# Softmax denominators from products of ones with the transposed probabilities

## The reference, cut to what matters

```
q, k, v = heads(x @ Wq), heads(x @ Wk), heads(x @ Wv)       # 8 heads of 32
scores  = einsum('bhnd,bhmd->bhnm', q, k) / sqrt(32)
scores  = where(adj, scores, -inf)
attn    = softmax(scores, axis=-1)
out     = relu(einsum('bhnm,bhmd->bhnd', attn, v)) @ Wo
x       = layernorm(x + out)
```

## Time and profile before

| | |
|---|---|
| median of three runs | 1895.2 us (1893.5 to 1897.09) |
| span of the profiled execution | 1892.0 us, 40139 instructions |
| mean granted TensorE clock | 0.963 of full speed |
| PE busy | 1672.9 us (88%) |
| DVE busy | 1513.0 us (80%) |
| ACT busy | 1120.7 us (59%) |
| POOL busy | 1314.4 us (69%) |

### The profile page before, as it was taken

One profiled execution on the slowest core, in us unless ns is written; L12 is line 12 of the kernel. 1 busy time (PEld: TensorE's weight loads), 2 busy tenths in 40 slices (PEclk: granted clock), 3 DMA queues, 4 the chain that ended last, 5 costly groups with the idle time before them and its releaser, 6 DMA issues.

```text
span 1892.0 us, 40139 instructions
## 1 busy us (share of the span) xinstructions
PE 1672.9 (88%) x12032; PEld 1482.6 (78%) x12032; DVE 1513.0 (80%) x5366; ACT 1120.7 (59%) x2718; POOL 1314.4 (69%) x1690
## 2 busy tenths in 40 slices
PE   5999999965999999999899999999989898989895
PEld 4777777754888888888788888888878787878784
DVE  3888888877788778788887887887888888888873
ACT  3888888864556556556465565565554545554542
POOL 3355555534787787787777877877868787888786
PEclk8999999996999999999899999999999898999998
DMA  5233333323121121121211211211212122212101
GB/s 181 63 89 89 89 89 89 89 79 123 34 67 58 42 67 58 42 67 54 91 56 44 67 52 47 67 53 47 67 34 68 64 70 65 68 64 69 63 26 45
DMA packets 150477, 127.31 MB, mean 67 GB/s; under 512 B 14880, under 2 KB 143392, under 8 KB 150432
## 3 DMA queue, kind: packets, MB, share of 16 engines
q1 hardware_dynamic: 145024, 124.30, 21.4%
q10 hardware_dynamic: 5408, 2.50, 0.5%
HBM read 89.03 MB, written 37.75 MB: 67 GB/s over the span
## 4 chain that ended last, share of the span: by engine, by line
PE 24%; DVE 20%; POOL 19%; issue 11%; ACT 3%; POOLq 1%; DVEq 0%; ACTq 0%
PE ps L45 14%; PE ps L819 6%; POOL gnn_norm L154 5%; DVE gnn_junk L913 5%; PE ps L795 3%; DVE gnn_small L929 2%; POOL gnn_norm L742 2%; POOL gnn_h L746 2%; POOL xo L761 2%; POOL gnn_norm L757 2%; POOL inv L149 2%; DVE gnn_small L934 2%; DVE gnn_small L937 2%; DVE gnn_res L972 1%; DVE gnn_st L976 1%
## 5 line engine op out<-in xcount | busy, mean ns | idle before, releaser
L819 PE MATMUL ps<-gnn_w_hi,gnn_g_hi 128*128 128x256 f32 x1536 | 454.8, 296 | 41.7 <-DVE gnn_res L972 41.0
L819 PE MATMUL ps<-gnn_w_lo,gnn_g_hi 128*128 128x256 f32 x1536 | 445.7, 290 | 0.0
L819 PE MATMUL ps<-gnn_w_hi,gnn_g_lo 128*128 128x256 f32 x1536 | 444.9, 290 | 0.0
L141 POOL TENSOR_TENSOR fence_pool<-half_neg 128x1 f32<-128x1 f32 x304 | 64.1, 213 | 477.3 <-DVE gnn_mv L1063 169.0
L980 DVE TENSOR_TENSOR gnn_g_lo<-ps,gnn_g_hi 128x512 fp32r<-128x512 f32 x384 | 263.1, 685 | 135.3 <-ACT ps L893 135.2
L892 ACT ACTIVATE gnn_g_hi<-ps,b_cols 128x512 fp32r<-128x512 f32 x384 | 264.5, 689 | 179.4 <-PE ps L45 155.3
L819 PEld LDWEIGHTS ps<-gnn_w_hi,gnn_g_hi 128*128 128x128 f32 x1536 | 305.6, 199 | 47.5 <-DVE gnn_res L972 44.8
L45 PE MATMUL ps<-gnn_hT_hi,gnn_w_hi 128*128 128x512 f32 x768 | 333.4, 434 | 4.0 <-DVE gnn_g_lo L980 4.0
L869 ACT ACTIVATE gnn_e<-gnn_u,gnn_small 128x128 f32<-128x128 f32 x192 | 74.9, 390 | 400.3 <-DVE gnn_small L938 400.3
L819 PEld LDWEIGHTS ps<-gnn_w_lo,gnn_g_hi 128*128 128x128 f32 x1536 | 306.7, 200 | 1.9
L819 PEld LDWEIGHTS ps<-gnn_w_hi,gnn_g_lo 128*128 128x128 f32 x1536 | 305.8, 199 | 0.0
(11 more groups left out here) (116 smaller groups left out, 3925.2 us busy)
## 6 DMA issues: line engine op xcount, KB each, us to landing
hist<-xo SPq DMA_DIRECT2D x48, 512.0 KB, 3.3
x<-hist SPq DMA_DIRECT2D x48, 512.0 KB, 4.3
gmask<-mask_hist SPq DMA_DIRECT2D x48, 256.0 KB, 4.5
aw<-in_L_gnn_attn_w SPq DMA_DIRECT2D x48, 256.0 KB, 4.3
att_xq<-in_x SPq DMA_DIRECT2D x16, 512.0 KB, 4.8
att_xl<-in_x SPq DMA_DIRECT2D x16, 512.0 KB, 3.5
gnn_fin<-hist SPq DMA_DIRECT2D x16, 512.0 KB, 3.8
out<-gnn_fin SPq DMA_DIRECT2D x16, 512.0 KB, 2.8
```

The lines of the kernel that those rows point to most:

```text
L141: e.tensor_tensor(fence_pool[:, n:n + 1], half_neg[:, 0:1], half_neg[:, 0:1], ALU.add)
L819: mm = e.matmul(FF2[j % 2], g[a][:, m, j * N:(j + 1) * N], V[b][:, m, :], start=(n == 0), stop=(n == len(terms) - 1))
```

## The change

The denominators are no longer summed by the exponentials and no longer inverted as 128x8 values, spread and transposed. In their place PE multiplies a constant tile of ones (128x32) with the transposed probabilities of each head: each of the 32 rows that a head has in the output layout then holds the row sum for every node. These eight products go to PB[1], after both copies of probsT and ahead of the product with v. DVE takes the reciprocal of all 128x256 values out of PSUM into rdenT, ahead of att. ACT's copy of rdenT, DVE's small reciprocal and its spreading, and PE's two transposes go. The next graph's transposes into PB[1] wait for DVE's reciprocal where they waited for ACT's copy. The diff, without its lines for tensors, semaphores and the setting of ones:

```diff
                         e.wait_ge(exped, 2 * i + 1)
-                        e.wait_ge(rdenT_out, START + i)
+                        e.wait_ge(den_inv, START + i)
...
                         e.wait_ge(pT_out_b, i + 1)
-                        e.wait_ge(rden_out, i + 1)
-                        for k in range(KT):
-                            mm = e.transpose(PB[1][:, k * N:(k + 1) * N],
-                                             rden_cols[:, 4 * k:4 * k + 4].rearrange("p h d -> p (h d)"), ident[:])
-                        mm.then_inc(rdenT_made, 1)
                         e.wait_ge(pT_out_a, i + 1)
+                        for h in range(NH):
+                            rows = slice(DK * (h % 4), DK * (h % 4 + 1))
+                            mm = e.matmul(PB[1][rows, h // 4 * N:(h // 4 + 1) * N], ones[:],
+                                          probsT[:, h, :], start=True, stop=True)
+                        mm.then_inc(den_made, 1)
...
                         ins = e.activation(probs[b][:, h, :], probs[b][:, h, :], ACT.Exp, bias=neg_peak[b][:, h:h + 1],
-                                           scale=SCALE, accum_out=den[b][:, h:h + 1])
+                                           scale=SCALE)
...
-                        e.wait_ge(rdenT_made, i + 1)
-                        e.copy(rdenT[:], PB[1][:, 0:D].rearrange("p (k n) -> p k n", k=KT)).then_inc(rdenT_out, 1)
...
-                        e.wait_ge(exped, 2 * i + 2)
-                        e.reciprocal(rden[:], den[j % 2][:]).then_inc(den_inv, 1)
-                        e.wait_ge(den_inv, i + 1)
-                        e.tensor_copy(rden_cols[:], rden[:].rearrange("p (h o) -> p h o", o=1)
-                                      .to_broadcast([P, NH, DK])).then_inc(rden_out, 1)
...
-                        e.wait_ge(rdenT_out, START + i + 1)
+                        e.wait_ge(den_made, i + 1)
+                        e.reciprocal(rdenT[:].rearrange("p k n -> p (k n)"), PB[1][:, 0:D]).then_inc(den_inv, 1)
+                        e.wait_ge(den_inv, START + i + 1)
                         e.wait_ge(pv_made, i + 1)
```

More of the change, by code:

```diff
@@ L185, in gnn_kernel @@
             neg_peak = [sb(f"neg_peak{i}", [P, NH]) for i in range(2)]
-            den = [sb(f"den{i}", [P, NH]) for i in range(2)]
-            rden = sb("rden", [P, NH])
-            rden_cols = sb("rden_cols", [P, NH, DK])
+            ones = sb("ones", [P, DK])
             rdenT = sb("rdenT", [P, KT, N])
@@ L197, in gnn_kernel @@
             (masks_made, xT_made, xT_hi_out, xT_lo_out, proj_made, proj_out, s_made, scored, peaked, exped,
-             pT_made, pT_out_b, pT_out_a, pv_made, den_inv, rden_out, rdenT_made, rdenT_out, att_out,
+             pT_made, pT_out_b, pT_out_a, pv_made, den_made, den_inv, ones_set, att_out,
              attT_hi_out, attT_lo_out, wo_made, y_out, bn_out, eye_made, eye_added) = sems(
                 "masks_made", "xT_made", "xT_hi_out", "xT_lo_out", "proj_made", "proj_out", "s_made", "scored",
-                "peaked", "exped", "pT_made", "pT_out_b", "pT_out_a", "pv_made", "den_inv", "rden_out",
-                "rdenT_made", "rdenT_out", "att_out", "attT_hi_out", "attT_lo_out", "wo_made", "y_out", "bn_out",
+                "peaked", "exped", "pT_made", "pT_out_b", "pT_out_a", "pv_made", "den_made", "den_inv",
+                "ones_set", "att_out", "attT_hi_out", "attT_lo_out", "wo_made", "y_out", "bn_out",
                 "eye_made", "eye_added")
@@ L405, in body @@
                                       lambda w, k: w[:, 3, k, :]).then_inc(wo_made, 1)
+                e.wait_ge(ones_set, 1)
                 for k in range(KT):
@@ L420, in _ @@
             def _(e):
-                e.sem_inc(rdenT_out, START)
                 for n, w in ((2, Wv), (3, Wo)):
@@ L488, in _ @@
                 e.sem_inc(y_out, START)
+                e.sem_inc(den_inv, START)
+                e.memset(ones[:], 1.0).then_inc(ones_set, 1)
                 def split_weights(n):
```

## The result

The changed kernel takes 2003.93 us (median of 4 runs, 2003.34 to 2004.97) against 1894.84 us before: a ratio of 1.0577, 95% interval 1.0562 to 1.0592. It is slower by 109 us. Forecast were 1969 us and a range up to 2003.

What follows compares the result with a forecast made beforehand. PE was taken to set the pace in three graphs of four, DVE in the fourth; after the change, DVE's chain. 22.4 + 4R with R = 1.5 gives 28.4 us a group, 74 us more in all: 1969 us, range 1921 to 2003.

Steps and rivals of the forecast that it cites:

- the chain: Attention stage: copy to copy through DVE, 5.54 + R us for j = 0 to 2, 5.76 + R for j = 3.
- ACT's relief: ACT loses accumulator reads and the copy of rdenT, 1.0 us a graph; counted at nothing because ACT waits for PE.
- R: Time of DVE's new 128x256 reciprocal from PSUM, once a graph: taken as 1.5 us, ends 0.42 and 2.2.
- the clock: PE's granted clock in the stage: expected to stay 1.00; anything else would show the forecast wrong.
- Rival (a): Reciprocal at about an element a cycle, R = 0.42, PE keeps the pace: 30 us more, 1925 us; chance 0.17.
- Rival (c): ACT really paces the groups through copies freeing PE's banks; its 1.0 us a graph returns: 1861 us; chance 0.03.
- (d): Products of ones fit PE's wait, reciprocal lies beside the product with v, no net cost: 1895 us; chance 0.03.
- the two mean slopes: DVE reciprocal cost per element from small records: 4.3 and 5.7 ns, giving R = 1.26 and 1.61 us.
- 22.4 + 4R: Length in us of a group of four graphs through DVE: 28.4 with R = 1.5, against 23.78 before.
- y to the next copy: DVE link from residual y to the next graph's copy: y's 0.42 us, then 0.64 from L381 to the copy.
- 4.6 x 16: Attention stage's forecast loss: 4.6 us a group more, times 16 groups, 74 us.
- the 2.2 us: Upper end for the large reciprocal on DVE, from the longest 128x8 record at 8.1 ns an element.

Runs made afterwards that it cites:

- e3: Changed kernel with the accumulation of the exponentials put back on ACT, its sums unused: 2004.56 us, ratio 1.0590.
- e1: Changed kernel with DVE's large reciprocal replaced by a plain copy of the same 128x256 values, division left out: 1918.21 us, ratio 1.0136.
- e2: Changed kernel with the eight products of ones made twice in a row: 2029.19 us, ratio 1.0717.
- e4: Changed kernel with reciprocals of 1 to 256 values and some copies added at the attention stage's end, from PSUM and SBUF: 6.25 ns a value from 64 to 256.
- e11: Changed kernel with 24 more products of ones on PE at j = 3, ahead of the scores, which nothing reads: 1998.12 us, ratio 1.0551.
- e7: Changed kernel with the products of ones for heads 4 to 7 put ahead of PE's wait for DVE's copy: 2000.59 us, ratio 1.0564.
- e13: Changed kernel with both the diffs of e7 and e11: 1980.69 us, ratio 1.0463.
- e5: Kernel before the change, with denominators spread to 128x256 first and the reciprocal taken of all of them, instead of 128x8: 1987.84 us, ratio 1.0497.
- e12: Changed kernel with e11's 24 filling products and without POOL's four additions of the identity: 1993.02 us, ratio 1.0530.

## Why the prediction was wrong

**Right: the place and the mechanism.** The pace passes from PE to DVE, the chain is the one whose links were added up, ACT's relief is worth nothing (e3), the second network keeps its length. With R at its measured 1.757 the links give 7.30 us from copy to copy for j = 0 to 2 and 7.52 for j = 3; where neither POOL nor the clock lengthens it, the distance is 7.39 for j = 0 to 2, and for j = 3 it is 7.50 in many groups (about 7.77 in others, for a reason that is not shown). Rival (a), the pace with a short reciprocal, was put at 30 us; e1 measured 25. Rival (c) is refuted by e1, in which PE sets the pace, ACT keeps its relief and the kernel is still 25 us slower than before; e3 says the same of the changed kernel. (d) is refuted by e1 and e2.

**Wrong: the size of a term.** The step that failed first is the size of the reciprocal, "I take 1.5 us, between the two mean slopes". It is 1.757. By the forecast's own formula, 22.4 + 4R, the group would have been 29.4 us and the time 1985, which is inside the range; the terms below add the other 18 us. The extrapolation went over 32 times the size from two records 30 ns apart, and both ends of the bracket (4.3 and 5.7 ns) lay below the 6.25 that e4 shows. The large reciprocal lies on a line of 6.25 ns a value through the 128x1 of the earlier trace rows (159 + 255 x 6.25 = 1753); the 128x8 is 14 ns shorter than that line, and 14 ns over 7 values are 0.5 us over 255. Why it is shorter is not shown. The Trainium skill's rule of a repeat count of eight ("VectorE: DVE Perf Modes", "First, the fixed hardware budget"), read as eight steps, gave 2.3 us by the prediction's estimate. The measured 1.757 lies between 1.5 and 2.3: 6.25 ns a value are about six of the 1.05 ns that a copy takes for an element, so the trace does not bear out eight.

**Missing: three smaller terms** (hi and lo, y to the next copy, the clock), each from rows of the changed kernel or, for the clock, from e11.

| term | worked out | us |
|---|---|---|
| forecast | 4.6 x 16 | 74 |
| R 1.757, not 1.5 | 0.257 x 64 | +16 |
| hi and lo lengthened (336 and 510 ns in the mean, medians 294 and 426) | 0.126 x 64 | +8 |
| y to the next copy 1.22, not 1.06 (208.45 to 209.67) | 0.16 x 48 | +8 |
| stretches at half clock | changed kernel less e11 | +6 |
| products of ones to reciprocal 0.70, not 0.78 | 0.08 x 48 | -4 |
| sum | | 108 |
| measured | 2003.93 - 1894.84 | 109 |

On y to the next copy: the sum had y's length of 0.42 and then L381, but L379, its successor, starts 0.56 after y (208.45 to 209.01). The time between the end of one engine's instruction and the start of another's that waits for it was left out at this link; at the others it was inside the distance taken from the trace. The clock was named as what would prove the forecast wrong (a clock below 1.00) and not priced. Four of the five corrections have one sign: a link that isn't thought of makes a chain longer. The range's upper end of 2003 left no room for them beside its R of 2.0; the prediction had said that the 2.2 us would go into the range, and then ended it at a little over 2.0.

What stays open: why PE's wait of 2.4 us at j = 3, which stands in every group, is followed by half clock in five groups only (in e7 in nearly every one). e11 and e13 show that filling this wait removes the stretches; what picks the groups isn't shown. The length of this one wait does not decide it: e11's is still 1.06 us and no half clock follows up to the last group, while in e5 the wait for att is 1.10 us and PE runs at half clock behind it in some groups (0.50 from 212.1 to 214.0 us).

## What to carry to other kernels

A value that many lanes share should be inverted before it is spread: e5 and the kernel before differ by that order alone, 8 values or 256 under the same instruction, and by 94 us. When a resource without slack in its order takes over work from one that waits anyway (here DVE from ACT), work is taken off the path and put on it; look for who waits for whom before moving it. And where a term is extrapolated from small records, its upper bound belongs in the range together with a margin for links left out.

## What the runs showed of the hardware

- DVE's reciprocal takes 6.25 ns a value in each partition (1.70 us for 128x256 in a row of its own kind, 1.757 behind a wait), from PSUM as from SBUF; a copy of 128x256 out of PSUM takes 0.42.
- POOL's elementwise work lengthens some of DVE's instructions: hi from 0.29 to 0.53 and lo from 0.43 to as much as 0.66 us, and in the changed kernel each such long record lies beside L292's additions or the layer norm's L154. The att multiplication, which reads PSUM and SBUF, stays at 423 to 426 ns, and the reciprocal at 1745 to 1759. The Trainium skill, "SBUF — State Buffer", "SBUF: two separate sides", says that a POOL operation and a DVE operation in a two-port mode, or with two SBUF inputs while POOL's reads SBUF, exclude each other on one pair of ports. The trace agrees in which instructions are hit: the cast from SBUF (0.53 us) and the subtraction of two SBUF tiles (0.56 to 0.66); that the cast runs in a two-port mode no run here shows. With POOL's four additions gone, these two take 3.3 us less over the stage (e12).
- Filling PE's idle time with products that nobody reads made the kernel 5.8 us faster and left the distances of j = 0 to 2 as they were (e11); it made it 20 us faster where the stretches at half clock were frequent (e13 against e7, 2000.59 - 1980.69).
